# Value products of an attention stage done for two key tiles in a row

## The reference

```python
q = proj(x1t, Wq, bq)            # x1 = layernorm(x), x2 = ctx
k = proj(x2t, Wk, bk)
v = proj(x2t, Wv, bv)
scores = einsum('bhqd,bhkd->bhqk', q, k) / sqrt(16)
attn = softmax(scores, axis=-1)
out = einsum('bhqk,bhkd->bhqd', attn, v)
x = x + tanh(g_xattn[0]) * out'
x = x + tanh(g_ffn[0]) * (moe(rmsnorm(layernorm(x))) + shared_expert(...))
```

## Time and profile before

| | us |
|---|---|
| median of 3 runs | 1496.56 (1496.29 to 1497.58) |
| the profiled execution | 1503.05 |
| its span from first to last instruction | 1501.2 |
| PE busy | 1404.3 (94%) |
| VectorE busy | 999.0 (67%) |
| ScalarE busy | 875.5 (58%) |
| GpSimd busy | 861.9 (57%) |

### The profile page before, as it was taken

The page is one execution under the profiler, slowest core; times in us unless marked ns, Lnnn a source line. Parts: engine busy times, 40 slices in busy tenths (PEclk is TensorE's granted clock), DMA queues, the critical chain, the costliest instruction groups (busy, mean ns, idle before and its releaser), DMA issues.

```text
span 1501.2 us, 25163 instructions
## 1 busy us (share of the span) xinstructions
PE 1404.3 (94%) x7290; PEld 727.9 (48%) x7290; DVE 999.0 (67%) x2172; ACT 875.5 (58%) x1720; POOL 861.9 (57%) x1276
## 2 busy tenths in 40 slices
PE   5889999999999989999999999998899899999997
PEld 1223333333333333333333333277688787778886
DVE  5768888888888877888888888655654232323332
ACT  2467777777777767777777776734234333333332
POOL 6437667667677766777676763632212445555554
PEclk9899999999999999999999999999999999999999
DMA  5857677677767767776776765265453867775664
GB/s 141 194 136 202 179 194 197 177 196 190 170 175 186 192 168 173 179 195 177 192 188 167 181 168 129 89 211 134 113 198 86 240 146 157 187 185 111 113 113 78
DMA packets 183329, 247.93 MB, mean 165 GB/s; under 512 B 31045, under 2 KB 105420, under 8 KB 183198
## 3 DMA queue, kind: packets, MB, share of 16 engines
q1 hardware_dynamic: 160846, 208.42, 52.7%
q0 software_dynamic: 18256, 37.38, 13.1%
q10 hardware_dynamic: 4096, 0.53, 0.2%
HBM read 141.85 MB, written 103.88 MB: 164 GB/s over the span
## 4 chain that ended last, share of the span: by engine, by line
PE 52%; DMA 18%; issue 14%; POOL 5%; DVE 4%; ACT 3%; SPq 1%; POOLq 1%; ACTq 1%; another core or an unknown queue 0%; DVEq 0%
PE bank L1363 13%; PE bank L1320 11%; PE bank L1291 10%; PE bank L1269 9%; DMA arena<-m_rows 8%; DMA pv_d<-arena 4%; DMA out<-xs,ids 3%; POOL xs L743 3%; PE bank L1254 2%; PE bank L1307 2%; PE bank L1296 2%; ACT arena L1111 1%; DVE row_max L851 1%; PE bank L1258 1%; DMA arena<-pv_d 1%
## 5 line engine op out<-in xcount | busy, mean ns | idle before, releaser
L851 DVE TENSOR_REDUCE row_max<-bank 128x1 f32<-128x512 f32 x1024 | 674.9, 683 | 123.4 <-PE bank L1269 106.0
L1111 ACT ACTIVATE arena<-bank 128x512 f32<-128x512 f32 x1024 | 572.0, 608 | 247.5 <-PE bank L1291 224.3
L1291 PE MATMUL bank<-arena 98*128 98x512 bf16 x1024 | 391.8, 385 | 27.3 <-DMA arena<-m_rows 21.8
L1269 PE MATMUL bank<-arena 96*128 96x512 bf16 x1024 | 397.2, 390 | 18.6 <-DVE row_max L851 11.0
L1320 PE MATMUL bank<-arena 128*32 128x512 f32 x2048 | 275.9, 611 | 1.4 <-ACT arena L1111 1.1
L755 POOL DMA_INDIRECT out<-xs,ids x71 | 112.5, 1584 | 194.3 <-ACT xs L1195 148.9
L1291 PEld LDWEIGHTS bank<-arena 98*128 98x128 bf16 x1024 | 103.0, 101 | 202.4 <-ACT arena L1111 74.6
L1269 PEld LDWEIGHTS bank<-arena 96*128 96x128 bf16 x1024 | 101.1, 99 | 174.7 <-DVE row_max L851 90.7
L1363 PE MATMUL bank<-w_ring,h_hi 128*128 x568 | 184.1, 405 | 0.0
L1184 ACT ACTIVATE arena<-bank 128x256 f32<-128x256 f32 x103 | 39.5, 384 | 198.1 <-PE bank L1363 188.4
L644 POOL TENSOR_TENSOR arena<-arena 128x512 bf16<-128x512 f32 x62 | 71.5, 1152 | 138.6 <-ACT arena L1103 135.9
(11 more groups left out here) (174 smaller groups left out, 2002.2 us busy)
## 6 DMA issues: line engine op xcount, KB each, us to landing
arena<-parts_q SPq DMA_DIRECT2D x64, 256.0 KB
pv_d<-arena SPq DMA_DIRECT2D x32, 512.0 KB, 7.0
w_ring<-split_d SPq DMA_DIRECT2D x60, 256.0 KB
parts_k<-arena SPq DMA_DIRECT2D x96, 128.0 KB
arena<-parts_k SPq DMA_DIRECT2D x32, 384.0 KB
parts_q<-arena SPq DMA_DIRECT2D x96, 128.0 KB
arena<-in_w SPq DMA_DIRECT2D x36, 256.0 KB, 5.5
arena<-in_ctx SPq DMA_DIRECT2D x32, 256.0 KB, 3.1
```

Of the source, the lines that this page charges most:

```text
L851: nc.vector.reduce_max(row_max[b % 2][:, u:u + 1], m_ps[(STEPS * b + u) % M_BANKS][:], AX_X).then_inc(s_mx, 1)
L1111: nc.scalar.activation(probs[group % 3][:, j, :], e_ps[n % E_BANKS][:], ACT.Exp, scale=float(DH) ** -0.5).then_inc(s_exp, 1)
L1269: nc.tensor.matmul(m_ps[n % M_BANKS][:], q_stack[b % 3][0:STACK, h, qt * P:(qt + 1) * P], k_stack[b % 3][0:STACK, h, :], start=True, stop= ...
L1291: nc.tensor.matmul(e_ps[n % E_BANKS][:], k_stack[b % 3][0:SHIFTED, h, kt * P:(kt + 1) * P], q_stack[b % 3][0:SHIFTED, h, :], start=True, s ...
```

## The change

`values` gets the first of two pairs and does both, 8 products in a row, after one wait for the exponentials of the second. It stands at every eighth step (2, 10, 18, 26) instead of every fourth. No product is added or removed, and the order among the value products is the same.

```diff
-            def values(b, r):
-                g, kt = divmod(r, KT)
-                pair = 8 * b + r
-                pe.wait_ge(s_exp, STEPS * b + GROUP * (r + 1))
-                if r == 0:
+            def values(b, first):
+                g = first // KT
+                if first == 0:
                     pe.wait_ge(s_evac, 3 * b + 3)
-                if kt == 0 and pair:
-                    pe.wait_ge(s_u, pair // KT)
-                for j in range(GROUP):
-                    last = nc.tensor.matmul(pv_ps[2 * DH * j:2 * DH * (j + 1), :], v_ones[b % 3][:, kt, GROUP * g + j, :],
-                                            probs[pair % 3][:, j, :], start=(kt == 0), stop=(kt == KT - 1))
-                last.then_inc(s_pv, 1)
+                if first % KT == 0 and 8 * b + first:
+                    pe.wait_ge(s_u, (8 * b + first) // KT)
+                pe.wait_ge(s_exp, STEPS * b + GROUP * (first + 2))
+                for r in (first, first + 1):
+                    kt, pair = r % KT, 8 * b + r
+                    for j in range(GROUP):
+                        last = nc.tensor.matmul(pv_ps[2 * DH * j:2 * DH * (j + 1), :],
+                                                v_ones[b % 3][:, kt, GROUP * g + j, :], probs[pair % 3][:, j, :],
+                                                start=(kt == 0), stop=(kt == KT - 1))
+                    last.then_inc(s_pv, 1)
...
-                    if s % GROUP == VALUES_LATE:
+                    if s % (2 * GROUP) == VALUES_LATE:
                         if s < GROUP and is_b(i - 1):
-                            values(i - 1, STEPS // GROUP - 1)
+                            values(i - 1, STEPS // GROUP - 2)
                         if s >= GROUP and is_b(i):
-                            values(i, s // GROUP - 1)
+                            values(i, s // GROUP - 2)
...
-            values(B - 1, STEPS // GROUP - 1)
+            values(B - 1, STEPS // GROUP - 2)
```

## The result

The changed kernel takes 1544.51 us (median, 1542.05 to 1553.85) where the kernel before takes 1496.42. The ratio is 1.0315, with a 95% interval of 1.0277 to 1.0352: 48 us slower, where 37.5 were forecast. The profiled execution took 1545.74 us, 42.7 more than the one of before (1503.05).

What follows compares the result with a forecast made beforehand. PE was taken to set the pace, with VectorE 88% full behind it. Turns at +1.21 (19) and +1.62 us (12), with small corrections, summed to +38: 1541 profiled, 1534 as median, range 1512 to 1556.

Steps and rivals of the forecast that it cites:

- The border: Joined value groups: the second costs 0.88 us instead of 1.09, saving 0.21 per pair, four pairs a turn.
- rival (b): Only the borders count, stalls vanish in the DMA's wait: 27 us faster, 1470; chance 0.07.
- Rival (c): The second group of a pair saves nothing: 1556 us; chance 0.09.
- Step 22: Projection there, without its value group, waits for VectorE's m_rows: 0.85 us lost a turn, bounds 0.75 and 1.03.
- Step 7: Without step 6's value group, step 7 waits for the exponential of step 4: 0.42 us lost a turn.
- Steps 11 to 18: The router's products of step 14 stay in the middle as cover: nothing lost, upper end 0.3 us.
- Steps 27 to 2: Eight steps without any other product, held by the maxima: 5.28 us from step 27 to step 2's max_scores.
- A turn: Attention turn longer by 1.21 us in 19 turns that wait for the shift rows' DMA, 1.62 in 12 others.
- step 18: VectorE a little late there behind the router's copy: an estimated 0.1 us lost a turn.
- The landing: Shift rows' DMA lands for the next turn's step 0, 8.33 us after step 24; inside term +0.47 in 19 turns.
- PE's wait for the shift rows below 21.8: Sign expected at the turn's first score product: its waits for that DMA total less than 21.8 us.
- Rival (e): Added short waits lower the clock: if ten more turns fell, 30 us more, 1564; chance 0.05.

Runs made afterwards that it cites:

- after_half: The changed kernel with row_max over the first 256 of 512 keys only; 1.0114 of the kernel before.
- base2_p02: Kernel before, shift rows' DMA at step 22 not 24, denominators' reciprocal at 17 not 13, step 30's value group joined to step 2's; 1570.96 us, 1.0399.
- base2_p18: Kernel before, shift rows' DMA at step 22 not 24, denominators' reciprocal at 17 not 13, step 14's value group joined to step 18's; 1497.94 us, 0.9908.
- after_row22: The changed kernel with the shift rows' DMA issued at step 22 instead of 24; 0.997 of the kernel before.
- the two kernels with the early issue: The changed kernel and the kernel before, each with the shift rows' DMA at step 22 instead of 24; 1529.36 against 1504.38 us.

## Why the prediction was right, and where it was short

*Direction and cause held.* The value groups between the steps were the readers' time. Shown by after_half, which gives quiet turns all of it back, and by base2_p02 and base2_p18, which have one double group each and differ by 1.13 us in a quiet turn, according to the row of steps that is left without cover. The number has luck in it, as the terms show.

*The border.* Forecast 0.21 per pair by a double group of 1.88; measured 1.85 and 0.24 (2 x 1.09 - 0.09 - 1.85). The drain rule (Trainium skill, TensorEngine Tiling (Array Packing), Key Properties) was no more than this gain, and rival (b), which went by it alone, is out: 1470 against 1544. Rival (c) is out by the same row.

*Step 22.* Forecast 0.85 (0.75 to 1.03), in all 20 to 25 us; the rows show 0.80 and 19.6.

*Step 7.* Forecast 0.42, measured 0.30. *Steps 11 to 18*: forecast nothing, measured slightly less than that, since the router's products no longer stand behind a value group (300.94 to 301.75, 0.81 instead of 0.91).

*Steps 27 to 2.* Forecast 5.28 us, measured 5.23.

*A turn.* I had +1.62 for a turn without a landing wait and +1.21 for one with it. Quiet turns have +1.11: each small term came out better than forecast (0.12 for the four borders, 0.12 at step 7, 0.1 each at step 18 and at the router's products). The busy ones, in which most landings fall, have +1.59, but that is not the banks' doing alone. In the 20 busy turns the clock is at its lower level for 48 us after and 14 before; half of the difference is 0.85 a turn, which leaves about 0.74. The seven busy turns that are at full clock in both traces, six of them with a landing wait before, are 0.81 longer in the mean. So both kinds of turn came out 0.4 to 0.5 below the forecast, and the change cost less in turns with a landing wait, as forecast.

*The landing.* "PE's wait for the shift rows below 21.8" and "the change makes the longest wait shorter" did not come: 21.6 us in 18 places, the longest 2.9 as before. I had held the landing fixed at 8.33 us from step 24 and let the longer row eat into the wait, 0.41 us a turn in 19 turns. But the DMA itself took longer: from its issue to the product that waited for it 7.08 us in the mean of the 19 places before and 7.39 in the 18 after.

*The clock, the term that failed.* Rival (e) had 0.05 and my sum had nothing for the clock. It came: 11 places instead of 5, about 13 us of the 39.2, a third. Before, a wait of 1.52 us was passed at full speed. After, a wait of 1.14 us was not. PE's timeline at that turn's end:

```profile
723.82 0.39 PE L1291 MATMUL bank<-arena 98*128 98x512 bf16 x1 [0.23 <-ACT arena L1111]
724.40 0.39 PE L1269 MATMUL bank<-arena 96*128 96x512 bf16 x1 [0.19 <-DVE row_max L851]
725.93 0.39 PE L1291 MATMUL bank<-arena 98*128 98x512 bf16 x1 [1.14 <-DMA arena<-m_rows]
726.15 0.52 PE L1269 MATMUL bank<-arena 96*128 96x512 bf16 x1
726.46 0.63 PE L1291 MATMUL bank<-arena 98*128 98x512 bf16 x1
```

PE was idle for the banks just before, 0.23 and 0.19, then for the landing, and products went from 0.38 to 0.63. Nine of the ten falls at the end of a turn in this trace stand beside a wait for the landing with bank stalls ahead of it. The page of the Trainium skill that I had weighed against the trace (TensorE: Matmul & The Clock Gate, A second HAM failure mode: psum-queue depth-cycling) tells of short idles that bring the clock down; the trace of after_row22 agrees with it, by the six falls behind stalls of 0.18 to 0.30 us alone. What decides at one place and not at another is open: the same stalls were passed at full clock in most turns.

*The sum.* For the profiled execution I had +38 and it is +42.7: turns 0 to 30 39.2 (forecast 37), the last turn, up to the first product of the shared expert, 4.3 (16.36 to 20.68; forecast 1; two double groups at the lower clock took 3.38 and 3.26 there instead of 1.92, 2.8 us more), the remainder -0.8. Of the 39.2 about 13 are the clock's, so the banks, borders and step 22 gave about 26 where 37 were forecast, in line with the 25 us between the two kernels with the early issue. That the sum came so near is luck: the mechanism was right, its terms were about 11 us too large, and the clock, priced at nothing, filled the gap. The last 5.4 us of the 48.1 are in the base: the profiled execution of before was 6.6 over its median, that of the changed kernel 1.2.

## What to carry to other kernels

When small groups of work stand between the steps of a chain with few buffers, they are the readers' catching-up time: before moving one, count the steps that are left in a row, and hold banks and readers' pace against them. Moving work changes three other distances as well: from a maximum to the operation that needs it, from the issue of a DMA to its use, and from a store to the load behind it in the same queue; here the first held a projection for 19.6 us in all. And it opens stalls that are short by themselves but, many in a row or ahead of a longer wait, can bring the clock down; here that was about a third of the loss. Joining groups of another array shape is a real gain, of 0.24 us a pair, where the row that grows has other work in its middle and no late DMA in its readers' lists.

## What the runs showed of the hardware that was not expected

The kernel before took 1496 us in one comparison, 1531 in two others and 1512 in the fourth, with a mean granted clock of 0.981 where it took 1496 (in the trace), 0.970 at 1531 and 0.977 at 1512. The cause is not shown; the spread is larger than many of the differences here, so only kernels of one comparison can be held against each other. A 16-matmul double group at the lower clock took 3.20 to 3.44 us and 1.92 at the higher. The clock fell behind bank stalls of 0.18 to 0.30 us alone, in six turns of one trace. A wait of 1.52 us was passed at full clock in one place (the kernel before), and one of 1.14 us was not in another (the changed kernel, with bank stalls of 0.23 and 0.19 us ahead of it).
